# The negated row maxima of an attention layer turned by VectorE's block transpose and sent through DRAM, in place of a TensorE transpose

## What is computed

```
q_lr = einsum('bhtd,hdr->bhtr', q, Wq_lsr)
k_lr = einsum('bhtd,hdr->bhtr', k, Wk_lsr)
scores = einsum('bhir,bhjr->bhij', q_lr, k_lr) * scale
scores = where(causal_mask, -inf, scores)
attn = softmax(scores, axis=-1)
y = einsum('bhij,bhjd->bhid', attn, v)
```

## Time and profile before

| | |
|---|---|
| median of 3 runs | 1021.04 us (1019.87 to 1022.62) |
| the profiled execution | 1019.15 us |
| its span, first to last instruction | 1017.3 us |
| mean granted TensorE clock | 0.959 of full speed |
| TensorE matmul busy | 916.4 us, 90% of the span |
| VectorE busy | 782.7 us, 77% |
| ScalarE busy | 588.7 us, 58% |
| GpSimd busy | 340.1 us, 33% |
| main DMA queue | 60.7% of 16 engines' span |

### The profile page before, as it was taken

How to read it: one execution, slowest core, us unless ns; L and a number is a source line. 1 busy time by engine, 2 the same in 40 slices (tenths; PEclk the granted TensorE clock), 3 DMA queues, 4 the chain that set the end, 5 groups by cost and what they waited for, 6 DMA issues and landing times.

```text
span 1017.3 us, 25757 instructions
## 1 busy us (share of the span) xinstructions
PE 916.4 (90%) x9572; PEld 722.5 (71%) x9572; DVE 782.7 (77%) x1693; ACT 588.7 (58%) x1121; POOL 340.1 (33%) x571
## 2 busy tenths in 40 slices
PE   3567999999999999999999999999999999998863
PEld 3445677777777777777777777777777777776652
DVE  4336788888888888888888888888888888778542
ACT  1114556776666666667666666666766666546642
POOL 8001222333333333233433333333333333222332
PEclk9679999999999999999999999999999999989876
DMA  5876766777766656667777666666777766610000
GB/s 174 148 125 127 134 123 128 132 141 142 142 121 106 115 130 128 127 127 141 142 141 130 109 105 131 127 130 123 141 141 143 141 111 100 124 33 29 22 11 22
DMA packets 114792, 118.69 MB, mean 117 GB/s; under 512 B 20649, under 2 KB 98283, under 8 KB 114667
## 3 DMA queue, kind: packets, MB, share of 16 engines
q1 hardware_dynamic: 114667, 117.03, 60.7%
HBM read 74.00 MB, written 41.94 MB: 114 GB/s over the span
## 4 chain that ended last, share of the span: by engine, by line
PE 41%; DVE 30%; issue 10%; ACT 9%; POOL 9%; DMA 1%; SPq 0%; DVEq 0%; POOLq 0%; ACTq 0%
PE ps_m L486 14%; PE ps_m L478 7%; DVE row_max L865 4%; PE ps_s L499 4%; POOL xT_lo L1076 4%; DVE s_neg L962 4%; PE ps_m L449 3%; ACT p L673 3%; PE ps_m L616 3%; DVE bn L882 3%; DVE yu L899 2%; PE ps_t L499 2%; PE ps_m L600 2%; PE ps_s L514 2%; POOL rstd L1064 2%
## 5 line engine op out<-in xcount | busy, mean ns | idle before, releaser
L865 DVE TENSOR_REDUCE row_max<-ps_s 128x4 f32<-128x1024 f32 (+1 forms) x192 | 233.3, 1215 | 37.0 <-PE ps_s L514 33.3
L673 ACT ACTIVATE p<-ps_t 128x1024 f32<-128x1024 f32 x192 | 196.9, 1025 | 29.1 <-PE ps_t L514 28.3
L1061 POOL TENSOR_TENSOR var<-mv,eps 128x2 f32<-128x2 f32 x96 | 18.9, 197 | 466.8 <-DVE mv L888 466.8
L499 PE MATMUL ps_s<-stack 48*128 48x128 f32 (+1 forms) x1024 | 108.6, 311 | 14.8 <-DVE row_max L865 11.1
L780 ACT COPY kxT<-ps_m 128x240 f32<-128x240 f32 x32 | 11.5, 359 | 175.9 <-PE ps_m L458 175.9
L499 PEld LDWEIGHTS ps_s<-stack 48*128 48x128 f32 x1024 | 72.7, 189 | 52.6 <-DVE row_max L865 28.4
L499 PE MATMUL ps_t<-stack 50*128 50x128 f32 (+1 forms) x1024 | 92.0, 279 | 9.5 <-DMA stack<-shift_parts 5.9
L560 PE MATMUL ps_o<-p,v_pad 128*32 128x256 f32 (+1 forms) x2048 | 96.3, 329 | 0.0
L560 PEld LDWEIGHTS ps_o<-p,v_pad 128*32 128x32 f32 x2048 | 57.4, 109 | 39.4 <-issue 17.4
L499 PEld LDWEIGHTS ps_t<-stack 50*128 50x128 f32 x1024 | 74.5, 190 | 11.4 <-DMA stack<-shift_parts 6.2
L1097 POOL TENSOR_TENSOR xr_lo<-dx,xr_hi 128x512 fp32r<-128x512 f32 x32 | 41.0, 1280 | 124.1 <-ACT xr_hi L743 124.1
(11 more groups left out here) (163 smaller groups left out, 2715.9 us busy)
## 6 DMA issues: line engine op xcount, KB each, us to landing
stack<-parts_dram SPq DMA_DIRECT2D x384, 128.0 KB, 6.0
parts_dram<-parts SPq DMA_DIRECT2D x64, 512.0 KB, 5.0
x_in<-in_x_turned SPq DMA_DIRECT2D x32, 256.0 KB, 4.4
x_res<-in_x SPq DMA_DIRECT2D x32, 256.0 KB, 4.5
out_x<-sum SPq DMA_DIRECT2D x64, 128.0 KB, 5.4
ctxT<-in_ctx_turned SPq DMA_DIRECT2D x32, 120.0 KB, 4.0
stack<-shift_parts SPq DMA_DIRECT2D x128, 8.0 KB
p<-in_Wq SPq DMA_DIRECT2D x1, 256.0 KB, 3.1
```

The lines of the kernel that those rows point to most:

```text
L499: nc.tensor.matmul(target[:, at_h:at_h + width], left[b.slot][r0:r0 + rows_n, h // 2, rows_at:rows_at + P], right[b.slot][r0:r0 + rows_n, ...
L673: nc.scalar.activation(p[c][:], ps_t[:], ACT.Exp).then_inc(exp_done[c], 1)
L865: nc.vector.tensor_reduce(row_max[:, tile, :, j0:j0 + nj], ps_s[:].rearrange("p (g j w) -> p g j w", j=nj, g=2), AX_X, ALU.max) \
```

## The change

The turn is made on VectorE and in DRAM. TensorE's two transposes and their turn of bank 0 are gone. row_max is laid out with the tile innermost, so that (head, tile) are 32 columns. While the tokens are still on the partitions, VectorE negates the 32 columns into a high part, makes the low part, and turns the 64 columns in blocks of 32 x 32 with its own transpose: partition 32 b + r then holds row r = (head, tile) for the 32 tokens of block b. All three instructions stand behind the last row maximum and ahead of the low part of k_act. SyncE writes the two parts to DRAM in the order (part, row, block, token), in pieces of 32 tokens, waits until they are there, and reads them back as the two rows of each half, 8 KB each: two writes and two reads instead of four copies.

```diff
-        row_max = sb("row_max", [P, NT, 2, HEADS // 2])
-        shift_parts = sb("shift_parts", [HEADS, 2, T], F32R)
-        shift = shift_parts[:, 1, :].bitcast(F32)
+        row_max = sb("row_max", [P, 2, HEADS // 2, NT])
+        shift_parts = sb("shift_parts", [P, 2, NT * HEADS], F32R)
+        shift_turned = sb("shift_turned", [P, 2, BLOCK])
...
+        shift_dram = [nc.dram_tensor(f"shift_dram{r}", [2, NT * HEADS, P // BLOCK, BLOCK], F32, kind="Internal").ap()
+                      for r in range(RING)]
...
-             ("mT", SCORES, v_["shift_done"]), ("z2", CROSS, v_["sum2_done"]), ("vx", PROBS, a_["vx_ready"])],
+             ("z2", CROSS, v_["sum2_done"]), ("vx", PROBS, a_["vx_ready"])],
...
-                    sp.wait_ge(v_["shift_lo"], c.n + 1)
+                    if c.n >= RING:
+                        sp.wait_ge(shift_loaded[c.slot], Batch(c.n - RING, IN).dma_count(2))
+                    sp.wait_ge(v_["shift_turned"], c.n + 1)
+                    for w in range(2):
+                        sp.dma_start(shift_dram[c.slot][w].rearrange("r b t -> b r t"), shift_turned[:, w, :]) \
+                            .then_inc(shift_saved[c.slot], 16)
+                    sp.wait_ge(shift_saved[c.slot], c.dma_count(2))
                     for g in range(2):
-                        for part in range(2):
-                            r0 = 64 * g + ONES_ROW + part
-                            sp.dma_start(stack[0][c.slot][r0:r0 + 1].bitcast(F32),
-                                         shift_parts[8 * g:8 * g + 8, part, :].bitcast(F32)).then_inc(shift_loaded[c.slot], 16)
+                        r0 = 64 * g + ONES_ROW
+                        rows_g = slice(HEADS * g, HEADS * g + HEADS)
+                        sp.dma_start(stack[0][c.slot][r0:r0 + 2].bitcast(F32),
+                                     shift_dram[c.slot][:, rows_g].rearrange("w r b t -> w (r b t)")) \
+                            .then_inc(shift_loaded[c.slot], 16)
...
                         if c == T_ORDER[0]:
-                            pe.wait_ge(shift_loaded[Pb.slot], Pb.dma_count(4))
+                            pe.wait_ge(shift_loaded[Pb.slot], Pb.dma_count(2))
...
-                if on[SCORES]:
-                    bank = bank_free(pe, "mT", at)
-                    pe.wait_ge(max_done[5], Sb.n + 1)
-                    for i in range(NT):
-                        last = nc.tensor.transpose(bank[0:HEADS, i * P:(i + 1) * P],
-                                                   row_max[:, i].rearrange("p g j -> p (g j)"), ident[:])
-                    last.then_inc(filled["f_mT"], 1)
                 PV(0)
...
                     if c == S_ORDER[0]:
-                        wait(dve, filled["f_mT"], Sb.n)
+                        wait(dve, v_["shift_lo"], Sb.n)
...
-                    nc.vector.tensor_reduce(row_max[:, tile, :, j0:j0 + nj],
+                    nc.vector.tensor_reduce(row_max[:, :, j0:j0 + nj, tile],
...
                 row_maxima(5)
                 if on[SCORES]:
-
-                    dve.wait_ge(filled["f_mT"], Sb.n + 1)
                     prev = Batch(at - 1, SCORES)
+                    maxima = row_max[:].rearrange("p g j i -> p (g j i)")
+                    dve.wait_ge(max_done[5], Sb.n + 1)
+                    nc.vector.tensor_scalar(shift_parts[:, 0, :], maxima, -1.0, None, ALU.mult) \
+                        .then_inc(v_["shift_hi"], 1)
+                    dve.wait_ge(v_["shift_hi"], Sb.n + 1)
+                    nc.vector.scalar_tensor_tensor(shift_parts[:, 1, :], maxima, -1.0, shift_parts[:, 0, :].bitcast(F32),
+                                                   op0=ALU.mult, op1=ALU.subtract).then_inc(v_["shift_lo"], 1)
+                    dve.wait_ge(v_["shift_lo"], Sb.n + 1)
                     if prev.n >= 0:
-                        dve.wait_ge(shift_loaded[prev.slot], prev.dma_count(4))
-                    nc.vector.tensor_scalar(shift, bank_of("mT")[0:HEADS, 0:T], -1.0, None, ALU.mult) \
-                        .then_inc(v_["shift_done"], 1)
+                        dve.wait_ge(shift_saved[prev.slot], prev.dma_count(2))
+                    nc.vector.transpose(shift_turned[:].rearrange("p w t -> p (w t)"),
+                                        shift_parts[:].rearrange("p w r -> p (w r)").bitcast(F32)) \
+                        .then_inc(v_["shift_turned"], 1)
                 if on[FFN]:
                     low_of(k_act_f32, k_act, "k_act_hi", "k_act_lo")
-                if on[SCORES]:
-                    dve.wait_ge(v_["shift_done"], Sb.n + 1)
-                    nc.vector.tensor_copy(shift_parts[:, 0, :], shift).then_inc(v_["shift_hi"], 1)
-                    dve.wait_ge(v_["shift_hi"], Sb.n + 1)
-                    nc.vector.tensor_tensor(shift_parts[:, 1, :], shift, shift_parts[:, 0, :].bitcast(F32),
-                                            ALU.subtract).then_inc(v_["shift_lo"], 1)
                 attention_out(0)
```

More of the change, by code:

```diff
@@ L26 @@
 VW = 32
+BLOCK = 32
 class Batch:
@@ L113, in decoder_layer @@
                for i, n in enumerate(raw_names)}
-        BLOCK = 32
         o_rec = sb("o_rec", [P, 2, 2, T // BLOCK])
@@ L171, in sems @@
             return {n: sem(n) for n in names}
-        filled = sems(*["f_" + n for n in ("q", "k", "v", "mT", "z1", "x1T", "s2", "g", "z2",
+        filled = sems(*["f_" + n for n in ("q", "k", "v", "z1", "x1T", "s2", "g", "z2",
                                            "kx", "vx", "x2T", "k3", "r3", "v3")])
@@ L190, in decoder_layer @@
         y_turned = [sem(f"y_turned{c}") for c in range(2)]
-        v_ = sems("yT_lo", "q_lo", "k_lo", "shift_done", "shift_hi", "shift_lo",
+        v_ = sems("yT_lo", "q_lo", "k_lo", "shift_hi", "shift_lo", "shift_turned",
                   "s2_max_done", "s2_neg_done", "s2_rec_done", "a_ready", "sum1_done", "sum2_done", "sum3_done",
@@ L205, in decoder_layer @@
         stack_loaded = [sem(f"stack_loaded{r}") for r in range(RING)]
+        shift_saved = [sem(f"shift_saved{r}") for r in range(RING)]
         shift_loaded = [sem(f"shift_loaded{r}") for r in range(RING)]
```

## The result

| | before | after |
|---|---|---|
| median of the runs (4 of each) | 1021.83 us | 1006.76 us (1005.62 to 1008.29) |
| the profiled execution | 1019.15 us | 1005.62 us |
| its span | 1017.3 us | 1003.9 us |

The ratio is 0.986, with a 95% interval from 0.9835 to 0.9885: faster, by 15.1 us in the medians and 13.5 us in the profiled executions. Forecast were 1005.5 us and, against the profiled execution's own time, 1004.35.

The account below looks back on a forecast made before the run. Bound: the 28.17 us loop through maxima transposes, VectorE's shift, GpSimd's low x and q. 29 x 0.51 = 14.8 us off 1019.15 gives 1004.35, by the median 1006.2; taken 1005.5, range 1000 to 1018.

Parts of the forecast that it names:

- TensorE's leg: Between g and PV(0): without two transposes and their bank, PV(0) starts 0.39 us earlier, bounds 0 to 0.63.
- PV(1) behind z2: Existing TensorE pair used for sizing: PV(1) starts 0.07 us before z2 ends, so PV(0) should follow g likewise.
- VectorE's leg: Three new instructions, 0.75 us, hidden before k_act_hi ends; attention-out transpose 0.55 us earlier, sum before the norm 0.51 earlier.
- What is late next: At the q projection: TensorE finishes its scores at 517.69, so GpSimd's x part is still late by some 0.3 us.
- The transfers: Shift's two writes and two reads through DRAM: rows land at 515.05, needed at 516.69, slack 1.6 us, cost nothing.
- the rule that the prediction sets against the change: Trainium skill on DMA: pieces under 512 bytes are read, changed, written back; some 2 us fixed cost, worst to DRAM.
- The slower rival: Shift rows land after 517.5 before next scores; step changes by landing minus 517.48; 1028 to 1109 us; 13%.
- The sum: Whole run: 29 steps x 0.51 = 14.8 us gained.
- The start-up: Three early steps without the last stage: new path about as long as the old, counted as nothing, within 1 us.
- VectorE alone: Rival: TensorE's own issue holds PV(0), only VectorE's tail shortens; 0.17 us a step, 1014 to 1016 us; 10%.
- The third rival: Shift rows land between 517.2 and 517.6 and eat the gain: 1018 to 1024 us; 7%.
- The late row: Shift rows land too late for the next scores: slower, 1028 to 1109 us, 13%; gain eaten, 1018 to 1024, 7%.

Follow-up runs that it names:

- 1: Changed kernel with two unread transposes of a constant put back between g and PV(0), with the shared bank's wait for tanh: period 28.07 us, 1017.04 us.
- 2: Changed kernel with two unread transposes of a constant ahead of PV(0), written to its own bank ps_o without a bank wait: period 27.87 us, 1012.64 us.
- 8: Changed kernel with GpSimd's low part of x moved ahead of the second norm's small steps: period 27.66 us, 1006.12 us.
- 5: Changed kernel with one more DRAM-to-DRAM trip (two transfers and a wait) between the shift's writes and reads: mean period 28.2 us, 1025.55 us.
- 6: Changed kernel with two more DRAM-to-DRAM trips between the shift's writes and reads: mean period 32.9 us, 1180.03 us.
- 7: Kernel before the change with GpSimd's low part of x moved ahead of the second norm's small steps: period 29.12 us, 1049.44 us.
- 9: Changed kernel with GpSimd's sum of x1 and bias waiting until VectorE has scaled the cross-attention's maxima: period 27.41 us, 999.06 us.

## Why the prediction was right

**TensorE's leg.** PV(0) right behind g, 0.39 us earlier: measured 0.38, and shown by 1 and 2 to be two halves, work and wait. PV(1) behind z2 was the right row to size it by.

**VectorE's leg.** The three instructions took 0.18, 0.19 and 0.24 us, 0.61 where I had 0.75, and 0.68 with the hand-overs, hidden under k_act_hi as written. The copy and the subtraction are off the path. The sum in front of the norm came 0.49 earlier, where I had 0.51.

**What is late next: wrong.** "TensorE must be there by then: it finished the first scores at 517.67 + 0.41 = 518.08, now 517.69." That is the row of ps_s's masks. Behind them TensorE issues those of ps_t. The timeline of the kernel before has both, and q behind them:

```profile
517.67 0.41 PE L514 MATMUL ps_s<-mask_s,identb 64*64 64x512 bf16 x4
...
517.91 0.39 PE L514 MATMUL ps_t<-mask_t,identb 64*64 64x512 bf16 x4
...
518.48 0.35 PE L478 MATMUL ps_m<-xT_hi,hi_Wq 128*128 128x256 f32 x1 [0.17 <-POOL xT_lo L1076]
```

TensorE finished at 518.30. In the changed kernel q follows the same masks by 0.08 us (508.11 and 508.19 in the chain), so before it could have started at 518.38, 0.10 ahead of where GpSimd let it. The gain is TensorE's 0.39 and this 0.10, 0.49, and the period fell by 0.48. So TensorE was not 0.3 us ahead of GpSimd but 0.1, and after the change it is the bound (8: 27.66). That the forecast didn't suffer is luck: the 0.51 of VectorE's leg happened to be just about what TensorE's leg allowed.

A reading on the same point was wrong too. Of the 11.3 us that the prediction spreads over 28 waits for GpSimd, 0.40 each, 6.1 are one wait at 16 us, in the start-up; in the steady steps it is 0.17 each.

**The transfers.** "The row is there when it was", slack 1.6: right in direction, 2.3 us in truth. The issues are shorter than the 0.68 of the old ones (1.09 for two writes, 0.58 for two reads), the write takes 1.95 and not 2.3, the read 2.45 and not 2.2. So the rule that the prediction sets against the change is not borne out at this size: 128 pieces of 128 bytes landed in DRAM in 1.95 us, beside 1.92 for one 8 KB row of the old copy. At the start of the run, where TensorE really waits for it, one such write took 2.50. (The Trainium skill gives the 2 us, in DMA: Bandwidth & Descriptors, Anatomy of one DMA, for transfers that GpSimd issues; these are SyncE's.) The slower rival's law, that a step gets longer by what the landing passes the need, holds in 5's step with 0.45 us. Its threshold does not: on the old scale the rows landed at 516.69 + 0.45 = 517.14 there, for which "landing minus 517.48" gives a step of 27.83 us, and it took 28.1, since q has to wait for the masks of ps_t as well. Its price was too low too, as the clock falls on top of it (6).

**The sum.** 29 x 0.48 = 13.9 us against 29 x 0.51 = 14.8; the profiled executions differ by 13.5, the medians by 15.1. Over the whole profile most steps went from 28.15 to 27.68, which makes 13.6. The start-up counted as nothing: TensorE's two waits for the rows sum to 7.3 us there, 6.2 before.

**The rivals.** VectorE alone (0.17 a step): fell by 1, in which PV(0) stands where it was; what is left of the gain there is 0.10 a step and not 0.17, since TensorE is the bound at q there too. The third rival's price was added up wrongly: a landing at 517.2 makes 0.28 less a step by its own law, some 1013 us and not 1018. The late row, as loss or as a gain eaten: fell, with 2.3 us of slack, but it was nearer than 13% and 7% sound: one trip more made the kernel slower than before.

## What to carry to other kernels

Work that one engine does for another is worth moving if the new place lies in a wait that something else ends anyway: here 0.68 us in a gap of 1.19 cost nothing, while 0.39 on TensorE's own sequence, half of it a wait for a shared bank, was paid in each of 29 steps. When two legs meet, size both to their very last instruction, for the gain is the shorter of the two and the next bound is the other. A trip through DRAM of some 5 us was free here because it started early enough; find out its slack, and how much single trips differ, for beyond it TensorE may pay with its clock too.

## What was not expected of the hardware

- After 1.40 us of waiting, TensorE's granted clock was 0.57 from 360 to 368 us, and the same 12 matmuls took 2.86 instead of 1.63 us (5).
- A subtraction of VectorE with both inputs in SBUF took 1.39 instead of 0.41 us beside a GpSimd subtraction, and a tensor_scalar of 2 columns 1.25 instead of 0.17; moving either engine's instruction was worth 28 us in one case and 8 in the other (7, 9).
- Issuing a transfer of two rows of 8 KB out of DRAM took SyncE 0.27 us, one of 8 partitions by 1 KB from SBUF to SBUF 0.64.
